# FP4 weights turned by VectorE blocks during attention, the seam before the networks reordered, and the long passes of the tokens' FP4 rounding given to GpSimd

## The reference, cut to what matters

```python
xn = layernorm(x)
h  = rmsnorm(xn, attn_norm_w)
# 8 heads of 128, chunks of 128 tokens
attn = where(causal, q @ k.T, 0);  o = attn @ v + q @ S;  S = S + k.T @ v
x2 = xn + rmsnorm(o, out_norm_w) @ Wo
s  = x2 + (silu(h2 @ Wgate) * (h2 @ Wup)) @ Wdown      # h2 = rmsnorm(x2), inner width 1024
# FP4: per 16 elements, scale = max|.|/6, values rounded to the E2M1 grid, times scale
fp4_linear(a, w) = fp4(a) @ fp4(w).T
g  = silu(fp4_linear(silu(fp4_linear(xn, w_gate)) * fp4_linear(xn, w_up), w_down))   # inner width 704
out = x + s * g
```

## Time and profile before

| | |
|---|---|
| median of 3 runs | 1092.78 us (1090.03 to 1093.42) |
| the profiled execution | 1091.05 us, its span 1089.3 us |
| PE busy | 1066.1 us (98%) |
| PEld busy | 965.5 us (89%) |
| DVE busy | 929.4 us (85%) |
| ACT busy | 507.5 us (47%) |
| POOL busy | 50.7 us (5%) |
| DMA queue q1 | 147600 packets, 143.21 MB, 41.6% of 16 engines |
| mean granted clock of TensorE | 0.998 |

### The profile page before, as it was taken

One profiled execution on the slowest core, in us unless ns is written; L12 is line 12 of the kernel. 1 busy time (PEld: TensorE's weight loads), 2 busy tenths in 40 slices (PEclk: granted clock), 3 DMA queues, 4 the chain that ended last, 5 costly groups with the idle time before them and its releaser, 6 DMA issues.

```text
span 1089.3 us, 18698 instructions
## 1 busy us (share of the span) xinstructions
PE 1066.1 (98%) x6830; PEld 965.5 (89%) x6830; DVE 929.4 (85%) x1980; ACT 507.5 (47%) x1392; POOL 50.7 (5%) x70
## 2 busy tenths in 40 slices
PE   9999999999999999999999799999999999999997
PEld 6998999999998889999988689999989899989896
DVE  6888888998889888889768788888888888888896
ACT  6654645646546546465453623333333333333332
POOL 0000000000000000000000000101011010101010
PEclk9999999999999999999999999999999999999999
DMA  7455355453553554544435632242423233323122
GB/s 236 146 164 165 116 182 165 149 188 126 182 165 109 179 161 145 186 141 164 152 120 172 162 105 76 78 136 68 131 78 120 80 117 98 117 82 121 55 77 88
DMA packets 147691, 144.40 MB, mean 133 GB/s; under 512 B 11152, under 2 KB 142608, under 8 KB 147600
## 3 DMA queue, kind: packets, MB, share of 16 engines
q1 hardware_dynamic: 147600, 143.21, 41.6%
HBM read 77.94 MB, written 65.23 MB: 131 GB/s over the span
## 4 chain that ended last, share of the span: by engine, by line
PE 80%; DVE 12%; DMA 4%; ACT 2%; issue 1%; SPq 1%; POOL 0%; DVEq 0%; POOLq 0%
PE ps L257 61%; PE ps L668 5%; PE ps L709 4%; PE ps L703 4%; PE ps L689 4%; DMA moved<-work 2%; DMA r_gate<-moved 2%; DVE work L1495 1%; PE ps L620 1%; DVE r_v L1499 1%; DVE r_k L1433 1%; DVE work L1458 1%; DVE work L1454 1%; DVE r_v L1511 1%; DVE work L1506 1%
## 5 line engine op out<-in xcount | busy, mean ns | idle before, releaser
L257 PE MATMUL ps<-r_k,r_gate_up 128*128 128x512 f32 x768 | 189.4, 395 | 3.3 <-DVE work L1495 2.5
L257 PEld LDWEIGHTS ps<-r_k,r_gate_up 128*128 128x128 f32 x768 | 140.8, 189 | 35.5 <-DVE work L1495 8.1
L257 PEld LDWEIGHTS ps<-r_q,r_v 128*128 128x128 f32 x768 | 99.6, 192 | 9.7 <-DVE r_v L1499 4.6
L257 PE MATMUL ps<-r_o,onT 128*128 128x256 f32 x768 | 107.0, 288 | 0.1
L257 PE MATMUL ps<-r_q,r_v 128*128 128x256 f32 x768 | 104.0, 285 | 2.0 <-DVE r_v L1499 2.0
L1073 ACT ACTIVATE r_v<-work 128x512 fp32r<-128x512 f32 x64 | 40.5, 632 | 138.7 <-DVE work L1495 138.7
L934 ACT ACTIVATE work<-ps 128x128 f32<-128x128 f32 x256 | 67.2, 277 | 81.2 <-PE ps L709 81.2
L257 PE MATMUL ps<-hT,r_k 128*128 128x512 f32 x378 | 103.2, 408 | 0.0
L257 PE MATMUL ps<-hT,r_q 128*128 128x512 f32 x384 | 98.2, 391 | 0.0
L257 PE MATMUL ps<-r_v,hT 128*128 128x512 f32 x384 | 97.4, 390 | 0.0
L257 PEld LDWEIGHTS ps<-r_o,onT 128*128 128x128 f32 x768 | 95.7, 190 | 0.3 <-DVE onT L1213 0.3
(11 more groups left out here) (151 smaller groups left out, 1997.3 us busy)
## 6 DMA issues: line engine op xcount, KB each, us to landing
moved<-work SPq DMA_DIRECT2D x63, 512.0 KB, 2.9
r_gate<-moved SPq DMA_DIRECT2D x252, 128.0 KB, 2.5
kept_h<-work SPq DMA_DIRECT2D x31, 384.0 KB, 2.6
work<-kept_h SPq DMA_DIRECT2D x124, 96.0 KB, 2.3
work<-in_L_attn_hidden_states SPq DMA_DIRECT2D x16, 512.0 KB, 5.2
kept<-work SPq DMA_DIRECT2D x9, 514.0 KB, 4.6
kept_h<-work SPq DMA_DIRECT2D x9, 512.0 KB, 3.7
work<-kept SPq DMA_DIRECT2D x8, 514.0 KB, 6.2
```

What stands on the lines that cost most here:

```text
L257: done = pe.matmul(out_ap, a, b, start=first and n == 0, stop=last and n == 2, skip_group_check=skip)
```

## The change

1. Tokens' rounding: GpSimd makes the scaling, the addition, the subtraction and the scaling back; VectorE keeps maximum, factor and grid. Three new semaphores hand over (`x_factor_ready`, `x_scaled`, `x_grid_ready`), one orders GpSimd's own passes (`x_sum`). In the last block maximum and factor move to head 0, the grid to head 1, turning and storing to head 4.
2. FP4 weights: the pieces are now parts of the transposed matrix (order up, gate, down). Each is loaded so that 32x32 blocks lie where they belong once VectorE transposes each block (head 4 early): 4 DMAs per gate or up piece, 12 per down piece, in runs of 32 elements (128 bytes). The two up pieces get their halves straight away in blocks 1 and 2; the others are stored to `kept_w4` and loaded in the last steps or in the first network block. TensorE's transposes, the two memsets and the loads of `quant4` are gone.
3. The seam: gate_up4(0, 0), in other PSUM banks, and gate_up(0, 0) come ahead of the last out projection; Wdown's halves, the residual, the down weights' halves and x2_root move into the first network block.

```diff
+                for n in range(BLOCKS):                                  # gpsimd
+                    x_of_block = xn[:, n % HALVES, :, :].rearrange("p c d -> p (c d)")
+                    pool.wait_ge(x_factor_ready, n + 1)
+                    pool.tensor_tensor(x_groups(xq_new), x_groups(x_of_block), x_wide(2), ALU.mult)\
+                        .then_inc(x_scaled, 1)
+                    pool.wait_ge(x_grid_ready, n + 1)
+                    pool.tensor_tensor(xq_new, xq_new, grid_x, ALU.add).then_inc(x_sum, 1)
+                    pool.wait_ge(x_sum, 2 * n + 1)
+                    pool.tensor_tensor(xq_new, xq_new, grid_x, ALU.subtract).then_inc(x_sum, 1)
+                    pool.wait_ge(x_sum, 2 * n + 2)
+                    pool.tensor_tensor(x_groups(xq_new), x_groups(xq_new), x_wide(1), ALU.mult).then_inc(x_rounded, 1)
...
                 def early_extras(b, j, mine):
...
-                    if h == CH:
-                        fp4_max(xn[:, s, :, :].rearrange("p c d -> p (c d)"), x_scale, mine)
+                    if h == CH and rounds_piece:
+                        dve.transpose(h_flat[:, 0:PIECE4[n - 1]].rearrange("p (b t) -> p b t", t=QUAD),
+                                      piece.rearrange("p (b t) -> p b t", t=QUAD)).then_inc(piece_ready, 1)
+                    if h == (0 if final else CH):
+                        if n:
+                            dve.wait_ge(x_rounded, n)
+                        fp4_max(x_of_block, x_scale, mine)
+                    if h == CH and final:
+                        turn_xq(n)
                     if h == CH + 1:
+                        if rounds_piece and n <= KD:
+                            weights4_lo(n - 1, h_flat[:, 0:N4])
+                            dve.wait_ge(w4_ready, n)
+                        elif rounds_piece:
+                            dve.wait_ge(piece_stored, 16 * (n - KD))
+                        if final:
+                            dve.wait_ge(xq_stored, 16 * n + 16)
                         dve.wait_ge(h2_ready, n + 1)
                         dve.wait_ge(gu_ready, n + 2)
                         turn_blocks(h_flat, grid_x, h2_turned)
-                    if h == CH + 2:
-                        fp4_add(xq_new, grid_x, mine)
...
                 def late_extras(b, j, mine):
...
+                    if h == (0 if final else CH):
+                        if n:
+                            dve.wait_ge(xq_ready, n)
+                        fp4_factor(x_scale, mine).then_inc(x_factor_ready, 1)
...
-                    if h == CH:
-                        if n:
-                            dve.wait_ge(xq_ready, n)
-                        fp4_scales(xn[:, s, :, :].rearrange("p c d -> p (c d)"), xq_new, x_scale, mine)
-                    if h == CH + 1:
-                        dve.wait_ge(h2_turned, n + 1)
-                        fp4_grid(xq_new, grid_x, mine)
-                    if h == CH + 2:
-                        fp4_add(xq_new, grid_x, mine, ALU.subtract)
-                        fp4_scaled(xq_new, x_scale).then_inc(x_rounded, 1)
+                    if h == (1 if final else CH + 1):
+                        if not final:
+                            dve.wait_ge(h2_turned, n + 1)
+                        dve.wait_ge(x_scaled, n + 1)
+                        fp4_grid(xq_new, grid_x, mine, x_grid_ready)
+                    if h == CH + 2 and final:
+                        for k in range(KD):
+                            weights4_lo(KD + k, raw_gate4[:, k, :])
...
                     if h == CH + 1:                                      # sync, attention_transfers
...
-                            sp.dma_start(w4_piece, pieces_raw4[n]).then_inc(piece_loaded, 16)
...
+                    if h in (CH + 1, CH + 2) and n < PIECES:
+                        if n:
+                            sp.wait_ge(piece_ready, n)
+                        load_piece(n, range(QUADS // 2) if h == CH + 1 else range(QUADS // 2, QUADS))
...
+                            sp.dma_start(rows.rearrange("p (b e) -> p b e", e=QUAD), w[:, :, at:at + QUAD])\
+                              .then_inc(piece_loaded, 16)
...
                 pe.wait_ge(attn_ready, batches * STEPS)                  # tensor, the seam
                 pe.wait_ge(state_ready, batches * UPDATES)
-                for k in range(KD):
-                    turn_weights4(lambda f: raw_gate4[:, f, k * P:(k + 1) * P], k, W4_BANKS[k])
                 out_projection(H - 2, batches * STEPS - 1)
+                pe.wait_ge(w4_ready, 2 * KD)
+                gate_up4(0, 0)
                 turn_o(batches * STEPS)
-                pe.wait_ge(w4_loaded[1], 48)
...
+                pe.wait_ge(gu_ready, BLOCKS + 1)
+                pe.wait_ge(s_gate4_ready, 2)
+                gate_up(0, 0)
                 out_projection(H - 1, batches * STEPS)
...
+                    if h == CH and n0 + s in (1, 2):                     # scalar, attention
+                        weights4_hi(n0 + s - 1, h_flat[:, 0:N4])
...
-                x2_root(BLOCKS + 1)                                      # scalar, the seam
                 silu4(0, 0, (0,))
                 xT_hi_of(0, range(KD, TURNS))
                 silu4(0, 0, (1,))
+                last_o_hi(LAG + 1)
...
+                        if (n, c) == (0, 1):                             # scalar, networks
+                            act.wait_ge(onT_ready, batches * STEPS)
+                            act.wait_ge(down4_loaded, 32)
+                            for k in range(2):
+                                weights4_hi(4 + k, raw_down4[k])
                         hmT_hi(n, 2 * c)
...
                         hmT_hi(n, 2 * c + 1)
...
+                        if (n, c) == (0, 1):
+                            x2_squares(BLOCKS + 1)
+                            x2_root(BLOCKS + 1)
+                        if (n, c) == (1, 0):
+                            normed_h2(BLOCKS + 1, xq_new)
```

More of the change, by code:

```diff
@@ L217, in build @@
         two.at = v_at
-        raw_gate4 = two.cut(T4, D)
-        raw_up4 = [work[:, at:at + D] for at in (two.at, two.at + D, *range(0, (T4 - 2) * D, D))]
-        two.at += 2 * D
+        raw_gate4 = two.cut(KD, N4)
+        two.at = v_at + CH * BANK
         h2_in = two.cut(CH * D)
-        assert two.at <= v_at + 2 * CH * BANK
-        two.at = v_at + 2 * CH * BANK
+        x2b = two.cut(CH, D)
+        raw_down4 = [work[:, two.at - CH * D:two.at - CH * D + PIECE4[4]]]
+        assert two.at == v_at + 2 * CH * BANK
         xq_in = two.cut(CH * D)
-        s_gate = two.cut(TB)
+        two.at += CH * D
+        scale4 = two.cut(3, G4)
         hm = two.cut(TB)
-        raw_down4 = [work[:, down4_at:down4_at + N4P], two.cut(N4P)]
-        scale4 = two.cut(3, G4)
         assert two.at <= qT_at
@@ L233, in build @@
         res = two.cut(CH, D)
+        raw_down4.append(work[:, two.at:two.at + PIECE4[5]])
         g4 = two.cut(CH, D)
-        x2b = two.cut(CH, ROW)
-        two.at = max(two.at, x2_end)
+        two.at = x2_end
         h4_turned_sb = two.cut(QUADS, T4 * QUAD)
+        s_gate = two.cut(TB)
         hq_in = work[:, down4_at:down4_at + QUADS * T4 * QUAD].rearrange("p (a x) -> p a x", a=QUADS)
@@ L242, in build @@
         grid4 = two.cut(N4)
-        assert two.at <= v_at + (T4 + 2) * D and (T4 - 2) * D <= v_at
+        assert two.at <= v_at + CH * BANK
         ps = ctx.enter_context(nc.psum_tensor("ps", [P, 8, BANK], F32))
@@ new lines, in late_extras, with weights4_lo @@
+                    if h == CH + 2 and final:
+                        for k in range(KD):
+                            weights4_lo(KD + k, raw_gate4[:, k, :])
+                    if h == CH + 3 and n < PIECES:
+                        piece, scale, grid_w = w4_of(n)
+                        dve.wait_ge(piece_loaded, 16 * sum(piece_transfers(m) for m in range(n + 1)))
+                        fp4_max(piece, scale, mine)
+                        fp4_scales(piece, scale, mine)
+                def weights4_lo(m, turned_piece):
+                    i, k = PIECE_OF[m]
+                    dve.wait_ge(w4_hi, m + 1)
+                    hi, lo = halves4(m, HI), halves4(m, LO)
+                    if i == 2:
+                        turned_piece = turned_piece.rearrange("p (f n) -> p f n", n=D)
+                    if m < PIECES - 1:
+                        dve.tensor_tensor(lo, turned_piece, hi.bitcast(F32), ALU.subtract).then_inc(w4_ready, 1)
+                        return
+                    low, high, last = slice(0, REST4), slice(REST4, P), T4 // 2 - 1
+                    dve.tensor_tensor(lo[:, 0:last, :], turned_piece[:, 0:last, :], hi[:, 0:last, :].bitcast(F32),
+                                      ALU.subtract)
+                    dve.tensor_copy(lo[low, last, :], hi[low, last, :].bitcast(F32))
+                    dve.tensor_scalar(lo[high, last, :].rearrange("p (o n) -> p o n", n=P),
```

(11 more changed lines are left out.)

308 lines of the change are left out of this document (153 added, 155 removed).

## The result

The changed kernel takes 1133.39 us (median of 4 runs, 1133.24 to 1138.0) against 1092.57 us for the kernel before (4 runs, 1090.03 to 1093.42): a ratio of 1.0398, 95% interval 1.0376 to 1.042 (the two medians alone give 1.0374). It is slower. 1110 us had been predicted, with 1081 to 1131 as the range: the sign was right, the size less than half of what came, and the time lies just outside the range.

A forecast was written before the change was run, and what follows sets the result against it. TensorE was taken to bound the kernel, with VectorE having little air in attention. 1091.05 + 26.8 (holds) - 1.5 (old stalls) - 6.3 (seam) = 1110.0 us; range 1081 to 1131, the forecast's own 1100 to 1120.

The forecast's parts named there:

- What bounds the kernel: Attention: TensorE busy 517.6 of 519.1 us; VectorE later than about 1.4 us at heads 5 and 6 stalls it.
- GpSimd's pass, 2.54 us: One 1024-element pass on GpSimd: 0.14 us start plus four times 0.60 us work, read from one collision with VectorE.
- Which operations wait: From L1477's collision with a GpSimd pass (0.43 us lost): VectorE operations with two SBUF inputs wait for the whole pass.
- How many holds: Inverse root at head 5: L1159 and L1161 wait for GpSimd passes, L1160 may slip between; two holds, 2.1 us more.
- rival A: Head 5: GpSimd catches all three two-input steps; one more 2.65 us hold in eight blocks, +21, 1131 us; chance 0.20.
- The hold term: Attention, heads 4 and 5 (0 and 1 in block 7): VectorE's delays cost 2.8 to 4.4 us a block, +26.8 together.
- Old stalls swallowed, -1.5: Attention: the existing small TensorE stalls at the affected heads disappear inside the new delays, -1.5 us.
- Part 2, 128-byte loads at nothing: Weight pieces loaded in short runs at heads 5 and 6: charged 0 us, with 0 to 12 as bounds.
- rival C: The 128-byte loads are slow: +2 us in six blocks on top of the forecast, 1122 us; chance 0.07.
- Part 3, the seam: Between attention and networks: -10.7 for the earlier start, -1.4 for shed VectorE passes, +5.8 for ScalarE's gate wait; -6.3 us.
- B: Tiny VectorE operations don't wait for GpSimd, or its passes let them in; only the seam counts, 1083 us; chance 0.30.
- D: The holds are there, but VectorE's freed time hides most: within 3 us of now; chance 0.05.

The follow-up runs named there:

- experiment 7: Changed kernel with the tokens' four passes back on VectorE and the seam's squares and root one chunk later: 1085.45 us, ratio 0.9944.
- 10: Changed kernel with quarter passes, scaling and addition held until the head's normed output is written, squares and root one chunk later: 1086.01 us, ratio 0.9955.
- experiment 5: Changed kernel with each of GpSimd's four passes issued as four instructions of 256 elements: 1095.49 us, ratio 1.0049.
- experiment 4: Changed kernel with four extra TensorE matmuls ahead of the waiting ones in head 6 of blocks 0 to 6: 1125.63 us, ratio 1.0330.
- experiment 8: Changed kernel with GpSimd's scaling, addition and subtraction each waiting for the head's normed output, squares and root one chunk later: 1098.59 us, ratio 1.0070.
- experiment 2: Kernel before with only the four passes given to GpSimd, weights and seam as they were: 1132.17 us, ratio 1.0391.
- experiment 1: Changed kernel with the tokens' four passes back on VectorE, new weight pieces and seam kept: 1091.97 us, ratio 1.0025.

## Why the prediction was wrong, point by point

**What bounds the kernel.** Right. Attention had nothing to give, and VectorE's lateness of more than 1.4 us became TensorE's. That is why taking 4.9 us of passes from VectorE in each block bought nothing: in experiments 7 and 10 the work stands on either engine, for the same time.

**GpSimd's pass, 2.54 us: nearly right.** Measured 2.39 to 2.40 for addition and subtraction, 1.94 for the two scalings whose second input is broadcast. The step to it was not right: the collision's split into 0.14 of start and 0.60 of work is not what the sizes give. From 0.74 us at 256 elements (experiment 5's L594) and 2.40 at 1024 follow 0.55 per 256 elements and 0.19 us of start.

**Which operations wait.** The reading of the one collision as an exclusive wait for the whole pass was right, and so was the Trainium skill's sentence on it (SBUF — State Buffer, section SBUF: two separate sides); the runs agree, down to 4-element operations, which end 0.01 to 0.03 us after the pass. "Two inputs in SBUF" was too narrow: L1502 has one and is held too. That page names VectorE's two-port operations beside the two-input ones. I had quoted this and then counted the two-input ones only; no run here shows in which mode L1502 worked.

**How many holds: the step that failed first.** The prediction let L1411 (now L1502) by, and alternated GpSimd and the tiny operations so that two were held. In blocks 0 to 6 all three were, which is rival A. Its "for" was the right clue: L1411 was due within 0.2 us of the pass, and arrived 0.03 us after its start in blocks 0, 2, 4 and 6, 0.35 us after it in 1, 3 and 5. Only in block 7 did it slip by; there two were held, as forecast, and the step's 2.92 us is close to the sum's 2.8. With GpSimd's passes back to back every hold ends when a pass does, so the next candidate meets the next pass. What slips through is what comes in the gap between two passes (L1198, 0.16 us) or isn't held (the reciprocal). The hold term came to 33.5 us (the long steps of experiment 4, at full clock) where 26.8 stood: 4.18 to 4.51 in each of blocks 0 to 6 instead of 2.8 to 4.4. Rival A had priced the third hold at 2.65 x 8 = 21 us more. That was too much, and its 1131 us is near the measured time for a reason that is only half its own: the third hold and all errors of size made 6.7 us.

**The clock: the term that wasn't in the sum.** I had seen the half clock behind the 2.03 us wait in the seam and spoken of it there, but charged nothing for it in attention, where I had just forecast waits of 2 us in eight blocks. The waits were up to 3.6 us, and six stretches at 1.2 GHz came with them, 8.0 us in the long steps (experiment 4). This is somewhat more than the error in the holds. A forecast stall can have a second price, the slower matmuls behind it. When it falls due stays open: waits of 1.72 us (experiment 4, step 61) and 1.85 us (experiment 8, step 7) brought a stretch at half clock, and one of 3.34 us (block 3) didn't, so the length of the wait alone doesn't decide it. (Experiment 4 takes both away at once, the idle engine and the half clock.)

**Old stalls swallowed, -1.5: about right, but a term was missing.** With the passes alone on GpSimd (experiment 2) the last step starts 40.2 us later than before and the long steps make 41.5: 1.3 us were swallowed. In the changed kernel it starts 44.5 us later (636.83 against 592.30), so 3.0 us on top of the long steps' 41.5 are spread over small ones. With the passes back on VectorE something of this size is also there (experiment 1: 597.41, +5.1; experiment 7, with the same attention: 595.16, +2.9; so a single profile tells it to some 2 us), and it belongs to parts 2 and 3. Which instruction brings it stays open.

**Part 2, 128-byte loads at nothing: right.** 28736 packets are under 512 bytes where 11152 were, and TensorE waits for none of it; rival C falls. The rule of the Trainium skill that asks for 512 bytes a run (DMA: Bandwidth & Descriptors, section Specifications) isn't contradicted: the loads simply have more time than they need.

**Part 3, the seam.** Its two terms came out as worked: up to gate_up4(0,1) 33.5 became 21.9 us, a gain of 11.6 where 12.1 stood, and the wait for the SiLU behind two table loads (the third is before the first SiLU) cost 6.16 where 5.8 stood; the second half of gate_up4(0,2) starts 7.0 us earlier counted from the last step, against 6.3. What the sum had not: the half clock behind that wait took 2.6 us back (6.8 us at 0.5; gate_up4(0,3) is 4.4 earlier), one iteration of block 1 is 1.06 us longer, and the end another 1.0 later. Net -2.3 instead of -6.3. Again it is the clock, of which I had written that it could come back.

**The sum of what was missed**, on the profiled executions (1131.5 - 1089.3 = 42.2 against 19.0 forecast): holds 6.7, clock in attention 8.0, small steps 3.0 + 1.5 = 4.5, seam and networks 4.0; together 23.2. (They are shares of one measured total; that they add up proves nothing by itself.)

**The rivals.** B, no waiting, was given 0.30 and is refuted by the first timeline; D by the time. The range ended at A's 1131, with no room for A and the clock at once: two mechanisms that can both be true have to be added up for the range's end.

## What to carry to other kernels

Before work goes to GpSimd, look at which VectorE instructions stand right behind the one that triggers it: a 4-element step on the critical chain pays for a whole 1024-element pass, and giving VectorE less to do doesn't help where TensorE is the bound. If it must go, cut the passes into short instructions and start them behind the short chain, not in front of it (1133 to 1086 us here, with the root moved too). When a stall of some microseconds is forecast for TensorE, leave room in the range for the slower clock behind it (here six waits of eight brought it), and before an operation is moved on ScalarE count the table loads that it brings and who waits behind them.

## What the runs showed of the hardware that I had not expected

- A VectorE operation on 128x4 elements with a single SBUF input (tensor-scalar) lasts as long as the GpSimd pass beside it (2.39 us instead of 0.17), while reciprocal, masking, stream transpose and a product with a PSUM input keep their lengths beside GpSimd.
- A GpSimd product of 1024 elements a partition with a broadcast second input takes 1.94 us, a plain sum 2.40.
- With four useless matmuls in front of the wait, in seven of the eight blocks, the whole kernel is faster by 7.8 us: the clock stays at 2.4 GHz in those steps.
